# Cached attention in a one-core kernel: who issues which transfer of the attention stage

## The reference, cut to what matters

```python
B, S, HID = 64, 32, 512            # sequences, tokens, width
D, HQ, HK = 128, 32, 8             # head size, query heads, key/value heads
PAGES, PSIZE, NPP = 64, 32, 16     # pages in the pool, keys in a page, pages of a sequence
q, k, v = projections of x;  q, k = rope(rmsnorm(q)), rope(rmsnorm(k))
kc = k_cache[block_table]          # 16 pages of 32 keys per sequence
vc = v_cache[block_table]
k_all = concatenate([kc, k]);  v_all = concatenate([vc, v])      # 544 keys
scores = einsum(q, k_all) * SCALE, masked where the cache is not filled
o = einsum(softmax(scores), v_all);  result = o @ Wo.T
```

## Time and profile before

| | us |
|---|---|
| median of 3 runs | 3360.72 |
| the profiled execution | 3391.43 |
| its span (first to last instruction) | 3389.6 |
| TensorE busy in the span | 3121.2 (92%) |
| VectorE, ScalarE, GpSimd busy | 1770.8, 1498.1, 395.9 |
| mean granted TensorE clock | 0.962 |

### The profile page before, as it was taken

One profiled execution on the slowest core, in us unless ns is written; L12 is line 12 of the kernel. 1 busy time (PEld: TensorE's weight loads), 2 busy tenths in 40 slices (PEclk: granted clock), 3 DMA queues, 4 the chain that ended last, 5 costly groups with the idle time before them and its releaser, 6 DMA issues. The chain is left out here.

```text
span 3389.6 us, 94362 instructions
## 1 busy us (share of the span) xinstructions
PE 3121.2 (92%) x36400; PEld 2413.2 (71%) x36400; DVE 1770.8 (52%) x3389; ACT 1498.1 (44%) x3674; POOL 395.9 (12%) x1090
## 2 busy tenths in 40 slices
PE   8999998799988888989888799989999999699999
PEld 7888887566655566666556688867778788588884
DVE  4466667766656666666566444441333333344433
ACT  3455554566656666666566322211334333222210
POOL 0000001233222222322322000000000000200000
PEclk9999999899989999999999899999999999899999
DMA  5333332665555655555555534322333333643311
GB/s 189 111 107 106 93 106 82 185 187 184 183 164 166 187 172 167 176 173 183 179 167 175 165 115 122 111 77 100 118 110 94 94 111 92 177 124 116 107 38 50
DMA packets 526268, 454.40 MB, mean 134 GB/s; under 512 B 30562, under 2 KB 481634, under 8 KB 520931
## 3 DMA queue, kind: packets, MB, share of 16 engines
q1 hardware_dynamic: 525538, 450.98, 43.2%
q0 software_dynamic: 512, 0.26, 0.0%
HBM read 321.10 MB, written 130.02 MB: 133 GB/s over the span
## 5 line engine op out<-in xcount | busy, mean ns | idle before, releaser
L751 PE MATMUL ps_scores<-k_all,q_t 128*32 128x288 f32 (+1 forms) x8192 | 570.2, 423 | 153.8 <-DMA k_all<-kT_scratch 97.6
L701 DVE CUSTOM_DVE_ANT_0 masked<-ps_scores,reach,scale_now 128x544 f32<-128x544 f32 x512 | 391.7, 765 | 427.2 <-PE ps_scores L751 427.1
L766 PEld LDWEIGHTS ps_o<-weights_t,v_all 32*128 32x128 f32 x17408 | 520.7, 190 | 116.6 <-issue 114.9
L660 ACT ACTIVATE probs<-masked,shift 128x544 f32<-128x544 f32 x512 | 382.7, 748 | 448.7 <-DVE shift L701 448.4
L766 PE MATMUL ps_o<-weights_t,v_all 32*128 32x128 f32 x17408 | 569.3, 280 | 2.9 <-DMA v_all<-v_scratch 1.5
L751 PEld LDWEIGHTS ps_scores<-k_all,q_t 128*32 128x32 f32 x8192 | 253.9, 115 | 372.4 <-issue 199.7
L638 POOL COPY k_all<-k_pool 128x256 f32 x1024 | 354.6, 400 | 914.7 <-PE ps_scores L751 834.5
L714 DVE STREAM_TRANSPOSE weights_t<-probs 128x544 f32<-128x544 f32 x512 | 376.1, 735 | 21.3 <-ACT probs L665 6.7
L665 ACT ACTIVATE probs<-probs,inv 128x544 f32<-128x544 f32 x512 | 375.6, 734 | 0.0
L906 DVE TENSOR_TENSOR y<-y,s_ps 128x512 f32<-128x512 f32 x256 | 158.7, 681 | 375.9 <-PE s_ps L60 375.9
L865 ACT ACTIVATE s_h_hi<-s_h_raw 128x2048 fp32r<-128x2048 f32 x64 | 122.9, 1921 | 524.4 <-PE s_ps L60 517.1
(11 more groups left out here) (159 smaller groups left out, 4248.0 us busy)
## 6 DMA issues: line engine op xcount, KB each, us to landing
v_all<-vpool_in SPq DMA_DIRECT2D x1024, 128.0 KB, 2.3
qT_scratch<-turned SPq DMA_DIRECT2D x64, 512.0 KB, 3.2
q_t<-qT_scratch SPq DMA_DIRECT2D x64, 512.0 KB, 3.3
oT_scratch<-o_t SPq DMA_DIRECT2D x128, 256.0 KB, 3.4
s_h_raw<-oT_scratch SPq DMA_DIRECT2D x32, 1024.0 KB, 5.6
aT_scratch<-s_o_t SPq DMA_DIRECT2D x32, 1024.0 KB, 5.7
s_h_raw<-aT_scratch SPq DMA_DIRECT2D x32, 1024.0 KB, 5.7
w_raw<-w_in SPq DMA_DIRECT2D x12, 1024.0 KB, 6.1
```

The lines of the kernel that those rows point to most:

```text
L660: act.activation(probs[:, k % BUF, :], masked[:, k % 2, :], ACT.Exp, bias=shift[:, k % BUF:k % BUF + 1], scale=-1.0, accum_out=total[:, k ...
L701: dve.tensor_tensor_reduce(masked[:, k % 2, :], ps_scores[:, k % 2, LOW:LOW + KEYS], reach[:, k // HK, :], scale_now[:, k // HK, k % HK:k ...
L751: m = pe.matmul(ps_scores[q * S:(q + 1) * S, k % 2, cols], q_t[:, j, head, r * S:(r + 1) * S], k_all[:, j, pages, head * PSIZE:(head + 1) ...
L766: m = pe.matmul(ps_o[:, q, 0:GS], v_all[rows, j, t, e * D:(e + 1) * D], weights_t[rows, g, :, t * S:(t + 1) * S], start=t == 0, stop=t == NPP)
```

## The change

In `stage2` SP keeps only the 16 page loads of values per batch. GpSimd now issues the loads of q and of the own keys, the load of the own values and both output stores, between its own copies. Its order for each b is: wait for the scores of b, `load_qk(b + 2)`, `gather_k(b + 2)`, wait for the values of b-1, `load_v_own(b + 1)`, `store_o(b - 1, 1)`, `store_o(b, 0)`. Its loop now holds four batches. At the start it issues the q and key loads of batches 0 and 1 ahead of its first gather. The own values are kept in a new scratch tensor `v_pages` in the form of a page, so that one transfer of 128 rows of 1 KB fetches them; for that `stage1` stores each unit of values with two transfers of 256 columns in place of one of 512, and the rows of the value weight are reordered on the host.

```diff
# stage1, SP
-                        dst = scratch["v"][u * 2 * P:(u + 1) * 2 * P, cb * 512:(cb + 1) * 512].rearrange("(t p) n -> p t n", p=P)
-                        src = turned[:, u % 2, :].rearrange("p (t n) -> p t n", t=2)
+                        for h in range(2):
+                            dst = scratch["v_pages"][u * 2:u * 2 + 2, cb * 2 + h, :, :, :].rearrange("t q s n -> (q s) t n")
+                            src = turned[:, u % 2, :].rearrange("p (t h n) -> p t h n", t=2, h=2)[:, :, h, :]
+                            sp.dma_start(dst, src).then_inc(store_free[u % 2], 16)
+                        continue
# stage2, SP
+            for b in range(2):
+                for half in range(2):
+                    load_v_pages(b, b, half)
             def pair_of(i, first, last):
                 for j in range(2):
                     b = i * 2 + j
+                    if not (first and j == 0) and not (last and j == 1):
+                        sp.wait_ge(pv_done, b * 2)
+                        for half in range(2):
+                            load_v_pages(b + 1, 1 - j, half)
# stage2, GpSimd
+            def load_qk(b, slot):
+                pool.dma_start(q_t[:, slot, :, :], scratch["qT"][bass.ds(b, 1)].rearrange("o p h n -> p (o h) n")).then_inc(qk_loaded[slot], 16)
+                pool.dma_start(k_all[:, slot, NPP, :], scratch["kT"][bass.ds(b, 1)].rearrange("o p h n -> p (o h n)")).then_inc(qk_loaded[slot], 16)
+            def load_v_own(tile, q, slot):
+                pool.dma_start(v_all[:, slot, NPP, :], scratch["v_pages"][bass.ds(tile, 1), :, q, :, :].rearrange("o h s n -> (o h) s n")
+                                ).then_inc(v_own_loaded[slot], 16)
+            def store_o(b, e):
+                pool.wait_ge(o_copied, b * 2 + e + 2)
+                pool.sem_inc(pool_passed)
+                dst = scratch["oT"][bass.ds(b, 1), :, e * SEQ:(e + 1) * SEQ, :]
+                pool.dma_start(dst.rearrange("o p h n -> p (o h n)"), o_t[:, e, :, :].rearrange("p h n -> p (h n)")).then_inc(o_store_free[e], 16)
...
+            load_qk(0, 0)
+            load_qk(1, 1)
             pool.wait_ge(pool_loaded, 16 * (3 + TILES // 2))
             gather_k(0, 0)
             gather_k(1, 1)
+            for b in range(2):
+                load_v_own(0, b, b)
+            def four_of(i, first, last):
+                for j in range(SEQ):
+                    b = i * SEQ + j
+                    begun = not (first and j == 0)
+                    if not (last and j >= 2):
+                        pool.wait_ge(scores_done, b * HK + HK)
+                        pool.sem_inc(pool_passed)
+                        load_qk(b + 2, j % 2)
+                        gather_k(b + 2, j % 2)
+                    if begun and not (last and j == SEQ - 1):
+                        pool.wait_ge(pv_done, b * 2)
+                        pool.sem_inc(pool_passed)
+                        load_v_own(i + (j + 1) // SEQ, (j + 1) % SEQ, (j + 1) % 2)
+                    if begun:
+                        store_o(b - 1, 1)
+                    store_o(b, 0)
# stage2, TensorE
-                        pe.wait_ge(v_loaded[j], loads * V_DMAS + V_DMAS)
+                        pe.wait_ge(v_loaded[j], loads * 16 * NPP + 16 * NPP)
+                        pe.wait_ge(v_own_loaded[j], loads * 16 + 16)
```

More of the change, by code:

```diff
@@ L208, in _ @@
             for k in range(2):
-                sp.wait_ge(store_free[k], 16 + 16 * 12 * UN // 2)
+                sp.wait_ge(store_free[k], 16 + 16 * (2 * VU + 10 * UN) // 2)
             sp.wait_ge(const_loaded, 16 * (5 + 2 * SEQ))
@@ L278, in v_copy @@
                 act.wait_ge(proj_done, n + 1)
-                act.wait_ge(store_free[u % 2], n // 2 * 16 + 16)
+                act.wait_ge(store_free[u % 2], n // 2 * 32 + 16)
                 for t in range(2):
@@ L291, in block_of @@
                             root_of(cb + (u + 2) // UN, (u + 2) % UN)
-                    turn_copy(r, VU // 2 + i * UN + cb * (UN // 2) + u // 2, u)
+                    turn_copy(r, VU + i * UN + cb * (UN // 2) + u // 2, u)
                     if u < KC and not (kind == "k" and cb == 1):
@@ L555, in stage2 @@
         v_loaded = [hold(nc.semaphore(f"v_loaded{k}")) for k in range(2)]
+        v_own_loaded = [hold(nc.semaphore(f"v_own_loaded{k}")) for k in range(2)]
         k_gathered = hold(nc.semaphore("k_gathered"))
@@ L569, in stage2 @@
         block = hold(nc.Block())
-        V_DMAS = 16 * (NPP + SEQ)
         @block.sync
         def _(sp):
[L574 to L579, removed]
-                for half in range(2):
[L582 to L604, removed]
@@ new lines, in load_v_pages @@
+            def load_v_pages(b, slot, half):
+                first = half * NPP // 2
+                page = nc.values_load_multi_w_load_instructions(
+                    c["table"][0:1, bass.ds(b * NPP + first, NPP // 2)], engines=(mybir.EngineType.SP,), min_val=0, max_val=PAGES - 1,
+                    skip_runtime_bounds_check_because="the reference's indices lie in the pool")[1]
+                for k in range(NPP // 2):
+                    sp.dma_start(v_all[:, slot, first + k, :], a["vpool"][bass.ds(page[k], 1)].rearrange("o p n -> p (o n)")
+                                 ).then_inc(v_loaded[slot], 16)
@@ L643, in _ @@
             gather_k(1, 1)
[L645 to L650, removed]
+            for b in range(2):
[16 more added lines that the diff above has]
+                    store_o(b, 0)
+            four_of(0, True, False)
+            with pool.Fori(1, TILES - 1) as i:
+                four_of(i, False, False)
+            four_of(TILES - 1, False, True)
+            store_o(B - 1, 1)
+            for k in range(2):
+                pool.wait_ge(o_store_free[k], 16 * B)
         @block.scalar
@@ L668, in copy_o @@
                 act.wait_ge(pv_done, grp + 1)
-                act.wait_ge(o_store_free[slot], stores * 16 + 16)
+                if not isinstance(stores, int) or stores > 0:
+                    act.wait_ge(o_store_free[slot], stores * 16)
                 act.activation(o_t[:, slot, :, :], ps_o[:, :, 0:GS], ACT.Copy).then_inc(o_copied, 1)
@@ L1481 @@
     x = np.asarray(x).reshape(TOK, HID)
-    w1 = np.concatenate([np.asarray(L0_cond_Wv), np.asarray(L0_cond_Wq), np.asarray(L0_cond_Wk)], 0)
+    wv = np.asarray(L0_cond_Wv).reshape(2, SEQ, D, HID).transpose(1, 0, 2, 3).reshape(HK * D, HID)
+    w1 = np.concatenate([wv, np.asarray(L0_cond_Wq), np.asarray(L0_cond_Wk)], 0)
     wqkv = np.asarray(L0_attn_w_qkv)
@@ L1515 @@
         "v": nc.dram_tensor("v_scratch", (TOK, HK * D), F32).ap(),
+        "v_pages": nc.dram_tensor("v_pages_scratch", (TILES, SEQ, SEQ, S, 2 * D), F32).ap(),
         "oT": nc.dram_tensor("oT_scratch", (B, D, HK, GS), F32).ap(),
```

## The result

| | before | after |
|---|---|---|
| median | 3368.24 (4 runs, 3359.44 to 3382.5) | 3214.32 (4 runs, 3208.33 to 3219.02) |
| the profiled execution | 3391.43 | 3208.33 |
| mean granted clock | 0.962 | 0.980 |

The ratio is 0.9538, 95% interval 0.9494 to 0.9582: 4.6% faster. 3204 was forecast, 3165 to 3290 as range.

What follows compares the result with a forecast made beforehand. TensorE bounds attention without stalls; SP's issue chain delivers keys late. 3391.4 - 198.4 + 20 (loop heads) + 3.8 (start) + 2.5 (end) = 3219.3; the middle between 3189 and 3219 gave 3204 us, range 3165 to 3290.

Steps and rivals of the forecast that it cites:

- What bounds: Attention stage: without stalls TensorE is the bound, 16.32 us a batch; with stalls the kernel runs at 19.5.
- The keys late by SP's order: SP's queue in attention: own keys land at T + 21, wanted T + 16.3, T being the end of a batch's scores.
- Steady part: Attention from 663.8 to 1888.4, 1224.6 us; 1026.2 without stalls, 1026 to 1050 expected after the change.
- The loop heads: Head of TensorE's two-batch loop: 20 us of stalls kept there, bounds 0 and 88.
- the 198.4 us: Loss in attention's steady part: 139.6 us in 34 TensorE stalls, 58.8 us of slow running; at most all saved.
- rival 2: TensorE's loop heads stay: 88 us of long stalls remain in place of 20, total 3272; chance 0.14.
- 716.93: Time of a loop head in the earlier trace where TensorE stalled only 1.28 us, ended by keys; evidence against rival 2.
- c = 1.25: GpSimd's time per plain transfer in us, bounds 0.5 and 3.0; 12.8 us of work a batch, break at 1.96.
- The tightest chain: GpSimd's store of group 1 lands by T + 17.2, TensorE needs ScalarE's next copy at T + 20.4; 3 us.
- VectorE cannot hold GpSimd up: Attention stage: no hold-up of GpSimd by VectorE expected, as its 16 copies keep to 5.54 us.
- Start: Start of attention: four GpSimd transfers ahead of the first gather, 5.0 less 1.2, cost +3.8 us, bounds 1 and 11.
- 30.7 us excess: Profiled execution before, above the runs' median: if general, 3189 after; if in stalls that vanish, 3219; middle taken.

Runs made afterwards that it cites:

- sp_keys_first: Kernel before with SP issuing q and own keys ahead of output stores and value loads, nothing moved to GpSimd; 3284.99 us, ratio 0.9758.
- after_again: The changed kernel measured once more, unchanged; 3229.75 us, ratio 0.9616.
- stores_on_sp2: Changed kernel with both output stores put back on SP, behind the page loads; 3226.72 us, ratio 0.9517.
- pool_plus4: Changed kernel with four unused two-input GpSimd instructions behind each gather; 3318.75 us, ratio 0.9844.
- pool_plus8b: Changed kernel with eight unused two-input GpSimd instructions behind each gather; 3382.76 us, ratio 0.9995.
- pages_later2: Changed kernel with SP's page loads held back until two more heads of scores are done; 3244.23 us, ratio 0.9619.

## Why the prediction was right, step by step

- *What bounds.* Right. The clean batch of 16.32 us is the batch after (16.30).
- *The keys late by SP's order.* Right, shown by sp_keys_first. In the profiled executions it took 3391.4 to 3280.2, 111 us.
- *Steady part.* 1026.2 + 20 forecast, 1033.4 measured. The loop heads are the term that was mis-sized: 20 us kept, 6.6 in this execution (4.65 + 1.81 + 0.2), about 20 in after_again's, with three. The split of the 198.4 us is now about 111 for keys and 11 x 8 = 88 for loop heads. That 88 is also what I had priced as rival 2, but from the 17 stalls above 4.5 us, of which only 11 are fetches (one of 6.00 us, at 1774.73, is a wait for keys), so the two agree by chance. And I took it that the change would cure most of them, with no more reason than 716.93. In experiments that cure the keys alone they stay (3285, 3284, 3279), near rival 2's 3272. With all of the change they are rare, which is worth the other 50 to 70 us, over a third of the gain. Which part does that isn't settled, and so the cause of this share of the gain stays open: neither the keys' order, nor the page form, nor q and keys on GpSimd did it alone, stores_on_sp2 had 8 in one execution and lay at 3208 in another, and kernels with small regular waits of TensorE (pool_plus4, pool_plus8b) have 7 and 8. The forecast stood partly on luck here.
- *GpSimd.* c = 1.25 was taken, about 0.65 measured; 0.5 as lower bound was the near one. From the end of a batch's scores (1396.91) to the end of the first store (1405.87), and with the second store (0.54), GpSimd's work is 9.5 us a batch for 12.8; the sign of the slack was right, its size not. The nearest row (indirect transfers) was dearer per transfer. Landings: 3.4 us for keys and 5.2 for stores, 6.4 taken.
- *The tightest chain is the store of group 1.* Right where GpSimd is full: the wait is for output copies (pool_plus8b). With half of that load a wait for VectorE came ahead of it (pool_plus4).
- *VectorE cannot hold GpSimd up.* Right for transfers. But I looked only one way, at the large VectorE instructions, and missed `reach`: it is VectorE that waits for GpSimd, 1.1 us in the median batch. That is free here; in pool_plus4 TensorE waits for VectorE 36.5 us in the whole stage, 0.6 us a batch. The Trainium skill (SBUF — State Buffer, section Who interferes with whom) lists this kind of instruction (tensor_scalar with one input) among those that can take the shared ports, under conditions, and says that the later one waits for the whole instruction. The trace agrees that VectorE waits, but its wait lasts over several GpSimd instructions.
- *SP.* Its pages are never waited for, and it is idle 350 us from 700 to 1650, 6 us a batch; even 2 us later (pages_later2) they were in time.
- *Start.* +3.8 forecast, +2.1 measured (650.98 against 648.88). The four issues took 2.45 us, as c was half; less the 1.2, and GpSimd's first one went out at 642.85, 0.85 us later than SP's had.
- *End.* +2.5 forecast. From the last steady half to the next stage's first load it took 19.4 us for 15.0, +4.4, within the bounds.
- *Stage 1 and the rest.* 0 forecast. The attention stage's first VectorE instruction starts at 642.4 for 642.0, which is within the start's +2.1; the stages behind took +1.9 us.
- *Sum.* -191.2 + 2.1 + 4.4 + 1.9 = -182.8, and 3391.4 - 182.8 = 3208.6 (measured 3208.3). Half of the 30.7 us excess was taken off. The measured median, 3214, is near my case of an excess that lies in stalls (3219); the other executions of the kernel before have no trace, so where their difference lies is not shown.

## What to carry to other kernels

Where a late transfer stands behind others in an issuing queue, try the order of that queue first; here three moved lines gave over half of what a second issuing engine gave. Read stalls with no releaser by their place: if all stand at a loop head and packets of the instruction queue move in their idle time, they are fetches of the loop body; here a body twice as long made them certain. When an engine gets work at a new time, look at every instruction of its neighbour that shares its ports, the small ones too, and in both directions.

## What was not expected of the hardware

- GpSimd issues a plain transfer of 128 rows in 0.54 us and an own-value load in 0.71 (at most 0.82 in any of these kernels); SP takes 0.33 us and 0.2 between the earlier trace rows.
- A VectorE instruction of 0.445 us, started while GpSimd runs a row of copies, took 1.56 us, and 2.70 when more GpSimd work stood behind the row.
- A return of TensorE's loop cost 6.6 and 8.6 us in the two cases worked out here, with 9 packets of 16 KB in the instruction queue, in some passes of the same program and not in others; with a body twice as long there were 15 packets and a stall at all 14 returns.
